# A pre-norm attention and FFN block on one Trainium2 core: the opening in another order, and the attention loop written out

## The reference

```python
def layernorm(x, eps=1e-5):
    m = jnp.mean(x, -1, keepdims=True); v = jnp.var(x, -1, keepdims=True)
    return (x - m) / jnp.sqrt(v + eps)

# x: (4, 1024, 128) float32
def attn(x, W_qk, W_v, slope):              # one head of width 128
    s = jnp.einsum('bqe,bke->bqk', x @ W_qk, x) / np.sqrt(128)
    s = s + (kpos - qpos) * slope[0]
    s = jnp.where(qpos >= kpos, s, -jnp.inf)
    return jnp.einsum('bqk,bkd->bqd', softmax(s), x @ W_v.T)

def ffn(x, w_gate, w_up, w_down):           # int32 weights, 384x128, 384x128, 128x384
    wg, wu, wd = (w.astype(x.dtype) / 127 for w in (w_gate, w_up, w_down))
    return (silu(x @ wg.T) * (x @ wu.T)) @ wd.T

x = x + attn(layernorm(x), W_qk, W_v, slope)
x = x + ffn(layernorm(x), w_gate, w_up, w_down)
```

## Time and profile before

| | |
|---|---|
| median of 3 runs | 149.07 us (147.76 to 149.08) |
| profiled execution: span from its first to its last instruction | 146.2 us; the page gives no other time for it |
| instructions in the span | 4102 |
| PE busy | 126.0 us, 86% |
| DVE busy | 123.4 us, 84% |
| ACT busy | 111.5 us, 76% |
| POOL busy | 96.0 us, 66% |
| granted TensorE clock, mean | 1.000 |

### The profile page before, as it was taken

The page is one execution under the profiler, slowest core; times in us unless marked ns, Lnnn a source line. Parts: engine busy times, 40 slices in busy tenths (PEclk is TensorE's granted clock), DMA queues, the critical chain, the costliest instruction groups (busy, mean ns, idle before and its releaser), DMA issues.

```text
span 146.2 us, 4102 instructions
## 1 busy us (share of the span) xinstructions
PE 126.0 (86%) x1215; PEld 93.2 (64%) x1215; DVE 123.4 (84%) x341; ACT 111.5 (76%) x251; POOL 96.0 (66%) x157
## 2 busy tenths in 40 slices
PE   0259977999999999999999998969999899999922
PEld 0056565778877779868688866658756656675521
DVE  0749989997869996969997859999879899999972
ACT  4035689999867999759999649985699978898740
POOL 6490789953991536972339933798999999634530
PEclk9999999999999999999999999999999999999999
DMA  4895000000000000000000000000000221022204
GB/s 140 222 272 137 0 2 0 4 2 2 4 0 0 0 0 0 0 0 0 0 0 0 0 7 0 0 0 4 0 4 0 76 72 61 10 76 72 78 0 143
DMA packets 9806, 5.09 MB, mean 35 GB/s; under 512 B 449, under 2 KB 9793, under 8 KB 9793
## 3 DMA queue, kind: packets, MB, share of 16 engines
q1 hardware_dynamic: 9792, 4.92, 11.8%
HBM read 2.82 MB, written 2.10 MB: 34 GB/s over the span
## 4 chain that ended last, share of the span: by engine, by line
PE 49%; DVE 20%; POOL 13%; issue 6%; ACT 5%; DMA 3%; SPq 2%; DVEq 0%; POOLq 0%
PE work_ps L556 8%; PE attn_ps L571 5%; PE score_ps L504 5%; PE attn_ps L572 4%; PE attn_ps L573 4%; PE score_ps L506 4%; PE score_ps L505 4%; POOL hidden_lo L411 4%; DVE biased L841 3%; DMA wd_int<-in_L_ffn_w_down_dram 3%; DVE stats L726 3%; PE work_ps L504 3%; POOL xn L399 3%; POOL rstd L361 3%; DVE hidden L860 2%
## 5 line engine op out<-in xcount | busy, mean ns | idle before, releaser
L571 PE MATMUL attn_ps<-v_hi,probsT_hi 128*128 (+1 forms) x144 | 25.7, 219 | 3.3 <-DVE xs L851 2.2
L824 DVE TENSOR_TENSOR probsT_lo<-work_ps,probsT_hi 128x512 f16<-128x512 f32 (+3 forms) x48 | 25.1, 551 | 3.7 <-ACT probsT_hi L1007 3.3
L1007 ACT CAST probsT_hi<-work_ps 128x512 f16<-128x512 f32 (+3 forms) x48 | 21.6, 491 | 7.9 <-PE work_ps L556 7.7
L841 DVE CUSTOM_DVE_ANT_0 biased<-score_ps,bias,neg_score_scale 128x128 f32<-128x128 f32 (+7 forms) x32 | 25.7, 804 | 0.6 <-PE score_ps L506 0.6
L992 ACT ACTIVATE probs<-biased,neg_max 128x128 f32<-128x128 f32 (+7 forms) x32 | 25.1, 783 | 1.1 <-DVE neg_max L841 1.1
L573 PE MATMUL attn_ps<-v_hi,probsT_lo 128*128 (+1 forms) x144 | 25.7, 219 | 0.0
L572 PE MATMUL attn_ps<-v_lo,probsT_hi 128*128 (+1 forms) x144 | 25.7, 219 | 0.0
L556 PE MATMUL work_ps<-ident,probs 128*128 128x128 f32 x144 | 21.5, 275 | 0.2 <-DVE probsT_lo L824 0.2
L411 POOL TENSOR_TENSOR hidden_lo<-hidden,hidden_hi 128x512 f16<-128x512 f32 x13 | 16.2, 1262 | 7.7 <-ACT hidden_hi L1075 7.7
L437 POOL TENSOR_TENSOR xT_lo<-whole,xT_hi 128x512 f32 (+1 forms) x8 | 9.3, 1165 | 15.0 <-ACT whole L986 15.0
L556 PEld LDWEIGHTS work_ps<-ident,probs 128*128 128x128 f32 x144 | 16.5, 141 | 3.3 <-DVE probsT_lo L824 1.0
(11 more groups left out here) (135 smaller groups left out, 352.3 us busy)
## 6 DMA issues: line engine op xcount, KB each, us to landing
out_dram<-xs SPq DMA_DIRECT2D x7, 256.0 KB, 2.3
xs<-in_L_attn_x_dram SPq DMA_DIRECT2D x3, 512.0 KB, 7.6
xs<-in_L_attn_x_dram SPq DMA_DIRECT2D x2, 256.0 KB, 3.0
out_dram<-xs SPq DMA_DIRECT2D x2, 128.0 KB, 2.0
wgu_int<-in_L_ffn_w_gate_dram SPq DMA_DIRECT2D x1, 192.0 KB, 2.9
wgu_int<-in_L_ffn_w_up_dram SPq DMA_DIRECT2D x1, 192.0 KB, 3.1
wd_int<-in_L_ffn_w_down_dram SPq DMA_DIRECT2D x1, 192.0 KB, 4.3
wqk_in<-in_L_attn_W_qk_dram SPq DMA_DIRECT2D x1, 64.0 KB, 2.8
```

The source lines that it names most:

```text
L571: pe.matmul(attn_ps[:, 0:D], p_hi, v_j, start=(j == 0), stop=False)
L824: dve.tensor_tensor(probsT_lo[:, i % 2, cols], work_ps[:, bank, 0:n], probsT_hi[:, i % 2, cols], ALU.subtract).then_inc(work_emptied, 1)
L841: dve.tensor_tensor_reduce(biased[:, i % 2, 0:n], score_ps[:, i % 2, 0:n], bias[:, S - n:S], neg_score_scale[:, 0:1], 3.0e38, ALU.add, ALU ...
L1007: act.copy(probsT_hi[:, i % 2, CW * h:CW * h + n], work_ps[:, bank, 0:n]).then_inc(probsT_hi_ready, 1)
```

## The change

It does five things.

1. The moments of token tiles 0 to 3 are taken on DVE by seven small instructions (`first_moments`) as soon as these tiles' statistics exist; POOL does only the power, on 4 values for each partition (`first_rstd`). The statistics of tiles 4 to 7 come behind the maxima of the attention weights.
2. The order of the first row's pieces is xT0, q0, xT1, v0, q1, v1 in place of xT0, xT1, q0, q1, v0, v1; the scores of tiles 0 and 1 come right behind q0.
3. The preparation of the FFN weights goes behind the first scores: the casts on ACT behind the second exponential, the transposes on PE behind xT1 and behind q1, the maxima on DVE behind the split of q1, the scaling and rounding on ACT into tiles 1 to 4 of the first batch row, the `lo` part on POOL behind `norm(2)`.
4. The scores wait for q1 at tile 4, no more at tile 2.
5. The loops over batch rows 0 to 2 are written out on PE, ACT, DVE and POOL, without registers.

```diff
-    opening = prologue + [(0, 0)]
+    opening = [("xT", 0), ("q", 0), ("xT", 1), ("v", 0), ("q", 1), ("v", 1), (0, 0)]
...
@@ POOL
+            pool.wait_ge(first_var_ready, 1)
+            pool.tensor_tensor(first_rstd[:, :], first_var[:, :], norm_const[:, 4:5].broadcast_to([P, CT]), ALU.pow)\
+                .then_inc(first_rstd_ready, 1)
             norm(0)
...
-            with pool.Fori(0, B - 1) as b:
-                nxt = pool.snap((b + 1) % 2)
+            for b in range(B - 1):
+                nxt = (b + 1) % 2
...
                 norm(b + 2)
+                if b == 0:
+                    ffn_weights_low()
...
@@ PE
-                if i in (0, 2):
-                    taken(b - 1, ("q", i // 2))
+                if i in (0, CT):
+                    taken(b - 1, ("q", i // CT))
...
             turn_maxima(0)
             spread_powers(0)
...
-            turn_maxima(1)
+            keep_busy(4)
+            prologue_part(0, 0, *prologue[0])
             keep_busy(3)
-            prologue_part(0, 0, *prologue[0])
-            spread_powers(1)
-            prologue_part(0, 0, *prologue[1])
-            keep_busy(4)
             pe.wait_ge(attn_w_ready, 1)
             prologue_part(0, 0, *prologue[2])
-            prologue_part(0, 0, *prologue[3])
-            pe.wait_ge(ffn_w_copied, 3)
             scores(0, 0, 0)
             scores(0, 0, 1)
+            prologue_part(0, 0, *prologue[1])
+            turn_gate_up_weights()
             prologue_part(0, 0, *prologue[4])
             scores(0, 0, 2)
+            prologue_part(0, 0, *prologue[3])
+            turn_down_weights()
             prologue_part(0, 0, *prologue[5])
+            turn_maxima(1)
             transpose_probs(0, 0)
+            spread_powers(1)
+            pe.wait_ge(ffn_w_copied, 3)
             pe.wait_ge(w_pow_copied, 2)
-            with pe.Fori(0, B - 1) as b:
-                around(b, pe.snap(b % 2), pe.snap((b + 1) % 2), False)
+            for b in range(B - 1):
+                around(b, b % 2, (b + 1) % 2, False)
...
@@ DVE
+            def first_moments():
+                stat = stats[:, apart(0), 0:CT, :]
+                dve.tensor_tensor(first_sum[:, :], stat[:, :, 1], stat[:, :, 4], ALU.add)
+                dve.tensor_tensor(first_dif[:, :], stat[:, :, 1], stat[:, :, 4], ALU.subtract)
+                link(dve.tensor_tensor(first_square[:, :], stat[:, :, 2], stat[:, :, 5], ALU.add))
+                dve.tensor_scalar(first_mean[:, :], first_sum[:, :], 0.5, None, ALU.mult)
+                dve.tensor_scalar(first_within[:, :], first_square[:, :], 1.0 / D, EPS, ALU.mult, ALU.add)
+                link(dve.scalar_tensor_tensor(first_between[:, :], first_dif[:, :], 0.25, first_dif[:, :], ALU.mult, ALU.mult))
+                dve.tensor_tensor(first_var[:, :], first_within[:, :], first_between[:, :], ALU.add)\
+                   .then_inc(first_var_ready, 1)
...
@@ ACT, in around
+                    if b == 0 and i == 1:
+                        scale_gate_up()
+                    if b == 0 and i == 2:
+                        scale_down()
+                    if b == 0 and i == 3:
+                        gate_up_high()
+                    if b == 0 and i == 4:
+                        down_high()
```

More of the change, by code:

```diff
@@ L96, in emptied @@
         return pool_takes, around * per_round + (0 if pool_takes else len(opening)) + n
-    assert not any(by_pool(g) for g in middle[-NWORK:] + opening[-NWORK:])
+    assert not any(by_pool(g) for g in middle[-NWORK:])
     VECTOR_TAKES, POOL_TAKES = (len(opening) * (1 - k) + (B - 1) * sum(by_pool(g) == k for g in middle)
@@ L626, in keep_busy, with turn_gate_up_weights, turn_down_weights @@
                     pe.transpose(work_ps[:, NWORK - 1, 0:P], ident[:, :], ident[:, :])
+            def turn_gate_up_weights():
+                pe.wait_ge(ffn_w_float, 1)
+                for j in range(2 * HB):
+                    m = pe.transpose(gate_up_w_ps[j // HB][:, P * (j % HB):P * (j % HB + 1)], wgu_in[:, j, :], ident[:, :])
+                m.then_inc(ffn_w_turned, 1)
+            def turn_down_weights():
+                pe.wait_ge(ffn_w_float, 2)
+                pe.wait_ge(ffn_w_copied, 1)
+                for j in range(HB):
+                    m = pe.transpose(down_w_ps[:, P * j:P * (j + 1)], wd_in[:, P * j:P * (j + 1)], ident[:, :])
+                m.then_inc(ffn_w_turned, 1)
             pe.wait_ge(ident_ready, 1)
@@ L923, in _ @@
             bias_scores(2)
-            split_low(0, 0, *prologue[5])
+            split_low(0, 0, "q", 1)
+            ffn_maxima()
+            offer_maxima(1, 1.0)
+            split_low(0, 0, "v", 1)
+            take_exponents(1)
             split_probsT(0, 0)
+            take_powers(1)
+            offer_int_scale()
+            ffn_scales()
             for b in range(2, B):
                 dve.wait_ge(x_loaded[b], 16)
-            with dve.Fori(0, B - 1) as b:
-                around(b, dve.snap(b % 2), dve.snap((b + 1) % 2), False)
+            for b in range(B - 1):
+                around(b, b % 2, (b + 1) % 2, False)
             around(B - 1, (B - 1) % 2, B % 2, True)
@@ L1047, in _ @@
-            copy_high(0, 0, *prologue[3])
-            act.wait_ge(ffn_w_scaled, 1)
-            act.copy(gu_hi, gu_f)
-            exponentials(0, 0)
-            copy_high(0, 0, *prologue[4])
-            exponentials(0, 1)
-            copy_high(0, 0, *prologue[5])
-            copy_probsT(0, 0)
-            act.wait_ge(ffn_w_scaled, 2)
-            act.copy(d_hi, d_f).then_inc(ffn_w_hi_ready, 1)
-            with act.Fori(0, B - 1) as b:
-                around(b, act.snap(b % 2), act.snap((b + 1) % 2), False)
+            for b in range(B - 1):
+                around(b, b % 2, (b + 1) % 2, False)
```

106 lines of the change are left out of this document (63 added, 43 removed).

## The result

| | before | after |
|---|---|---|
| median of the runs, first comparison | 148.72 us (4 runs, 147.76 to 149.08) | 158.69 us (4 runs, 156.08 to 160.18) |
| median of the runs, second comparison | | 157.91 us (4 runs, 157.46 to 158.92) |
| span of the execution read here | 146.2 us | 156.3 us |
| instructions | 4102 | 3585 |
| PE / DVE / ACT / POOL busy | 86 / 84 / 76 / 66% | 82 / 79 / 71 / 63% |

The change makes the kernel slower: ratio 1.0575, 95% interval [1.0485, 1.0665], about 157.3 us; measured a second time it is 1.0611 [1.0529, 1.0693].

What follows compares the result with a forecast made beforehand. The prediction took PE to bound the steady attention, so its entry into that stream sets the end. +7.4 (opening) + 1.0 (ACT) - 1.5 (loops) = +6.9 took the span from 146.2 to 153.1, the time to 156.0 us; range 151.8 to 159.2.

Steps and rivals of the forecast that it cites:

- The first biasing: In the opening, the first biasing of scores starts at 15.3 us in place of 19.51, 4.2 us earlier.
- PE's new wait: In the opening, PE stands at the first FFN transpose for ACT's cast of gate and up weights: 3.3 us.
- The first weighing: PE's first weighing of v, its entry into the steady stream, comes at 31.0 us in place of 23.58: +7.4.
- ACT in row 0: Scalings and roundings moved into tiles 1 to 4 load ACT by 2.6 us; 1.0 reaches PE, bounds 0 and 2.6.
- The clock falls back: Rival: PE's thin stretch from 24.4 to 31.0 lets the stream begin at 1.2 GHz; 157.5 to 159.5 us, chance 0.18.
- The forecast's own case: Late first weighing, some ACT load and the loops' gain together give 154 to 157.5 us; chance 0.52.
- PE warms early: Rival: PE's clock rises during the stretch from 19.55, saving up to 2.4 us; 153.6 or 151.5 us, chance 0.17.
- From the span to the time: The runs' median lies 2.9 us above the profiled execution's span, unchanged, so span 153.1 gives 156.0 us.
- The loops: Writing out the attention loops removes gaps at v tiles and the loop's end: -1.5 us, bounds 0 and 3.5.
- POOL's FFN part: POOL's 2.6 us of FFN weight work goes behind norm(2), where POOL has room: costs nothing.
- The rival "faster": The opening's 4.2 us gain survives if casts cost PE nothing at the FFN transposes; 143.4 us, chance 0.08.

Runs made afterwards that it cites:

- e2: The changed kernel with both casts of the FFN weights put back as ACT's first work; 152.88 us, ratio 1.0243.
- e5: The changed kernel with ACT's scaling and rounding moved to tiles 6 and 7 of rows 0 and 1, POOL's part later; 154.96 us, ratio 1.0345.
- e7: The changed kernel with the edits of e2 and e5 together; 150.37 us, ratio 1.0163.
- e3: The changed kernel with 44 more identity transposes that nobody reads, put where PE waits in the opening; 153.61 us, ratio 1.0310.
- e4: The kernel before with only the early moments and DVE's opening order following them, loops kept; 148.31 us, ratio 1.0001.
- e1: The kernel before with its four attention loops written out, nothing else changed; 146.27 us, ratio 0.9811.
- e6: The changed kernel's early moments, early scores and written-out loops, with the FFN preparation in idle slots and ACT's scaling late; 147.04 us, ratio 0.9917.
- e9: e6 with batch row 1's statistics taken earlier on DVE and the small FFN scales behind the second biasing; 144.42 us, ratio 0.9758.

## Why the prediction was right, and what it mis-sized

The sign, the mechanism and the range were right: 156.0 us was forecast, with a range of 151.8 to 159.2, and 157.3 to 157.9 was measured. The steps one by one:

- **The first biasing**: forecast at 15.3, measured 16.15 (15.4 to 16.4 over the traces with the same opening). The weights' maxima waited 0.69 us for the load of `wv_in`, so they began at 6.02 and POOL's moments at 7.55, not 6.85. The power on four values, which had no row, takes 1.02 us against 1.65 on eight, in the gap between the bounds, and delays nothing.
- **PE's new wait** ahead of the transposes: forecast 3.3 us from ACT's cast, measured 3.16 from the same cast. e2 takes it away and gets 4.0 us back.
- **The first weighing**: forecast +7.4, measured +7.5. Two errors cancel: the opening began 0.85 us later than forecast, and the slow clock in the stretch of v0 and q1 ended within q1 (24.06) and not behind it. That the two agree so closely is luck of this execution: e5, with the same program up to there, has +8.5 (32.08), and the first trace +9.6 (33.20), both with a clock that was low for longer. What is left in e7, +2.8 without the wait, leads over the line of maxima and powers that the forecast placed there.
- **ACT in row 0**: forecast +1.0 between bounds of 0 and 2.6, measured about +2.3 (15.43 to 13.10 by e5). The term that was mis-sized is the reading of ACT's lead, "some 1 us of the 2.6 reaches PE". The changed kernel has ACT at 14.91 of 15 us from 35 us on, so nearly the whole load reaches PE. That it enters row 0 without the lead of a pipeline that has run for some time is a reading that no run tests.
- **The clock falls back**, a rival with a chance of 0.18: it came in part. The forecast's own case had the clock rise and stay. It rose at 24 and fell at 31 after PE had been busy for 1.97 of 5 us. e3, which keeps the clock up in the stretch of v0 and q1 too, prices the low clock at 1.4 us in round 0 and 1.6 ahead of it. The Trainium skill ("TensorE: Matmul & The Clock Gate", Part 1) has throttled as the default and activity as what releases it; the row 30 to 35 us agrees, granted 0.66 behind a thin stretch, and so does e3, in which no matmul of 512 columns behind 12.54 was slow.
- **PE warms early**, a rival with a chance of 0.17, came in a small part: the clock rose near 24, inside the stretch from 20.14 and not ahead of it. When it rises in the opening differs between executions: q's 512 columns took 0.63 us at 16.04 before, and 0.38 at 15.18 in e4. The rival's lower time doesn't add up either: 153.6 less 1.0 for ACT and 0.5 for the loops is 152.1 and not 151.5.
- **From the span to the time**: the forecast added 2.9 us, the distance of the median from the traced execution. In every execution on record that has both, the time is 1.7 to 2.0 us above its own span. The other 1 us is a difference between executions: those of the kernel before at a granted clock of 1.00 span 146.2 in the median, those below it 147.0. So the span was forecast 3.2 us short (153.1, measured 156.3), and the time only 1.9.
- **The loops**: forecast -1.5 between 0 and -3.5, measured -2.2 in this trace (rounds, row 3 and FFN together) and -2.7 in e1's median. Both places that were named, the v tiles and the loop's exit, show it. More than these two was gained, 0.3 of it in the FFN, which had no loop; where the rest comes from wasn't followed.
- **The tail**, +1.3, was in no term: a clock of 0.72 from 147.8 to 153.3. e1 has it as well (8.4 us against 7.28) and e2 and e7 don't (7.3), so the new opening is neither needed for it nor enough. What brings it is open.
- **POOL's FFN part** behind norm(2): forecast nothing. No wait of PE or DVE for it was seen; e5 moves it together with ACT's steps, so it wasn't tested alone.
- **The rival "faster"** held that the gain of the early scores survives. It fails as forecast, at the cast. e6 and e9 show that it isn't lost by nature: with the preparation in idle slots the first weighing keeps 1.65 us of it in e9.

In the spans ACT exceeds its term by 1.3, the opening by 0.1; the clock in round 0 (1.2, what ACT's 2.3 leaves of the 3.5) and the tail (1.3) had none; the loops gave 0.7 more than theirs. Together +3.2, which is 10.1 less 6.9. In the medians it is less, 157.3 to 157.9 against 156.0, for the reason given under the step from the span to the time.

## What to carry to other kernels

Side work that ran early, under another engine's long step, held nothing up here; moved "behind the critical part" of engines that take their instructions in order, it became part of the critical part, once for each queue that it stands in (PE's wait of 3.2 us, ACT's 2.3 in round 0, and the maxima and powers, to which most of 2.8 is put down). So look for the engines that wait while the critical one works, put it there, and put what is left where the same engine later shows gaps; then check who waits for what it displaced, as POOL did for 3.3 us in e6. And ask of each thinner stretch of PE what clock the stretch behind it will have.
